# Tap 0 of a causal convolution on VectorE from PSUM, and one 128x1024 subtraction on GpSimd

## The chip, the cores and the metric

The kernel runs on one core of a Trainium2 chip. The metric is the device time of one execution in microseconds (us). Three runs of the kernel before took 265.92, 267.05 and 267.52 us, median 267.05 us.

The engines are TensorE (PE, matmuls; its weight loads are PEld), VectorE (DVE), ScalarE (ACT), GpSimd (POOL) and SyncE (SP, which here only issues DMAs). Each has its own instruction queue and runs it in order; they wait for each other through semaphores.

## The reference

For `x` of 4 batches x 1024 tokens x 256 features, with `xn = layernorm(x)`, the result is `x + ssm(xn) + ffn(xn)`:

```python
xz = xn @ W_in.T                      # 256 -> 1024 = 512 (x_inner) + 512 (z)
conv[t] = sum(cw[k] * x_inner[t - 3 + k] for k in 0..3) + conv_b    # causal, per channel
x_conv = silu(conv)
s_C = x_conv @ W_x[16:].T             # 512 -> 16
h[t] = 0.95 * h[t-1] + x_conv[t]      # a scan over the 1024 tokens
y = h * (s_C @ exp(B_log).T) * silu(z)
ssm = layernorm(xn + y @ W_out.T) * ln_g + ln_b
ffn = quantise_fp6_blocks(xn) @ quantise_fp6_blocks(W_ffn).T + bias
```

The 512 inner channels lie in four chunks of 128 partitions; a chunk of a batch is a tile of 128 channels x 1024 tokens. Nearly all matmuls are done in two or three parts, with each factor split in a rounded `hi` and a remainder `lo = value - hi`.

## The kernel before, in words

Batches are software-pipelined. `step(s)` (one such function per engine) writes out by hand the order in which an engine works on batch `here = s`, on the next one (`nxt`) and on the tail of the previous one (`prev`). Steps run from -1 to 4; for batches that don't exist nothing is emitted. The order is static, so what stands first in an engine's queue and waits holds back all behind it.

For each chunk `c` of a batch the work around the change is this:

- PE: `x_half(c)` puts the chunk's `x_inner` in a PSUM slot (128x1024; there are three slots, `SLOT_X` and `SLOT_Z` say which), `z_half(c)` does the same for `z`. Before PE overwrites a slot, `slot_free` makes it wait for the last reader.
- ACT, `taps` (L613): L628 writes `xc = cw[3] * x + conv_b` from PSUM (tap 3), L632 writes `tap0 = cw[0] * x` from PSUM to a buffer in SBUF.
- DVE, `conv_tap` (L995, the instruction is L997): adds tap 2 and then tap 1 to `xc`, each as one `scalar_tensor_tensor` that reads the PSUM slot and `xc` and writes `xc`.
- POOL, `conv_tap0` (L391, L395): adds the shifted `tap0` buffer to `xc`; this sets `conv_ready`.
- ACT, `silu_x` (L644): SiLU of `xc` in place. DVE, `scan` (L1026): the recurrence, `xc` to `hy`. POOL, `gate` (L403): `hy *= silu(z)`; `silu(z)` lies in a single buffer `sz`, which ACT (L639) refills for the next chunk when the gate is done.
- When all four chunks have their SiLU, PE makes `s_product` (L812), ACT and DVE split its result (`s_low`, L1032), PE makes `cb_product`, and DVE `y_product` (L1039) multiplies it into `hy`.
- ACT `y_high` (L658) rounds `y`; the low part is `y_low`: on POOL for the chunks in `YLO_POOL = (0, 1, 2)` (L412), on DVE for chunk 3 (L1046), and in the last batch also chunk 1 on DVE (`MOVED`). PE `out_tile(t)` (t = 0 to 7, 128 tokens each; L839 to L857) multiplies out both branches of a token tile; the first of a batch waits for all four low parts at L857.

Other work in the same queues: DVE has the token statistics (L934, L942, L949, L950), the quantisation (`quantise`, L980; `block_max`, L959; `block_scale`, L967), the low parts `xn_low` (L986) and `xd_low` (L992), `take` (L1061 and L1063), which takes an output tile out of PSUM, and `finish` (L1076), the last addition, after which SP stores half a batch. POOL has `rstd_1` (L383, L387), `rstd_2` (L431 to L436), `dequantise` (L425) and `scale_g` (L454). ACT has `normalise` (L595), `norm_2` (L689), `squares` (L668), `xn_high` (L603), `xd_high` (L610).

Inputs of an instruction lie in SBUF, except for the PSUM slots and the two PSUM output banks (`obank`). So L997, L1039, L1032, L986, L992, L1061 and L1063 read one operand from PSUM and one from SBUF; L1026, L980, L1046 and L1076 read two from SBUF, and so do POOL's 128x1024 instructions.

Of the kernel before, what the change touches and what calls it, by code (L numbers as in the profile page):

```python
# [40 lines left out]
ALU = mybir.AluOpType  # L41
# [9 lines left out]

FP8_SHIFT = 64.0

YLO_POOL = (0, 1, 2,)


def wait(eng, sem, count):
# [6 lines left out]
def build(nc, x, w_in, conv_w, conv_b, w_x, b_log, w_out, ln_g, ln_b, ffn_w, ffn_b, out):  # L64
# [13 lines left out]
    with ExitStack() as ctx:  # L78
# [44 lines left out]
        xn_lo = sb("xn_lo", [P, KM, SEQ], F32R)  # L123
        xd_hi = sb("xd_hi", [P, KM, SEQ], F32R)
        xd_lo = sb("xd_lo", [P, KM, SEQ], F32R)
        tap0 = sb("tap0", [P, 2, SEQ])
        xc = sb("xc", [P, NCH, SEQ])
        sz = sb("sz", [P, SEQ])
        hy = sb("hy", [P, NCH, SEQ])
# [167 lines left out]
        def first(b):  # L297
            return b == 0
# [69 lines left out]
        def _(pool):  # L368
# [19 lines left out]
                                   ALU.mult).then_inc(nmr1_ready, 1)  # L388

            @of_batch  # L390
            def conv_tap0(b, c):  # L391

                wait(pool, tap1_done, NCH * b + c + 1)
                n = SEQ - (TAPS - 1)
                pool.tensor_tensor(xc[:, c, TAPS - 1:], xc[:, c, TAPS - 1:], tap0[:, c % 2, 0:n],  # L395
                                   ALU.add).then_inc(conv_ready, 1)

            @of_batch
            def gate(b, c):

                wait(pool, scan_done, NCH * b + c + 1)
                wait(pool, sz_ready, NCH * b + c + 1)
                pool.tensor_tensor(hy[:, c, :], hy[:, c, :], sz[:, :], ALU.mult).then_inc(hsz_ready, 1)  # L403
# [98 lines left out]

            def step(s):
                prev, here, nxt = s - 1, s, s + 1
                conv_tap0(here, 2)
                conv_tap0(here, 3)
                gate(here, 1)
                rstd_1(nxt, 0)
                gate(here, 2)
                rstd_1(nxt, 1)  # L510
                rstd_2(prev, 0)
                dequantise(here, 0)
                gate(here, 3)
                scale_g(prev, 0)
                if first(here):
                    centre_w_out()
                dequantise(here, 1)
                if first(nxt):
                    prepare_b()
                    prepare_bias()  # L520
                y_low(here, 0)
                if first(here):
                    w_out_low()
                y_low(here, 1)
                y_low(here, 2)
                rstd_2(prev, 1)
                conv_tap0(nxt, 0)
                scale_g(prev, 1)
                conv_tap0(nxt, 1)
                gate(nxt, 0)  # L530

            every_step(step)
# [5 lines left out]
        def _(act):  # L538
# [73 lines left out]
            @of_batch  # L612
            def taps(b, c):  # L613
                if first(b):
                    if c == 0:
                        for i in range(2):
                            act.wait_ge(conv_loaded[i], 16)

                    if c == 2:
                        act.wait_ge(b_ready, 1)  # L620
                    if c == 3:
                        act.wait_ge(bias_ready, 1)
                wait(act, x_ready, NCH * b + c + 1)

                wait(act, s_ready, b)
                wait(act, scan_done, NCH * (b - 1) + c + 1)
                src = slot[SLOT_X[c]][:, :]
                act.activation(xc[:, c, :], src, ACT.Identity, bias=cb[:, c:c + 1],  # L628
                               scale=cw[:, c, TAPS - 1:TAPS]).then_inc(taps_ready, 1)

                wait(act, conv_ready, NCH * b + c - 1)
                act.activation(tap0[:, c % 2, :], src, ACT.Copy, scale=cw[:, c, 0:1]).then_inc(taps_ready, 1)  # L632

            @of_batch
            def silu_z(b, c):
# [107 lines left out]
        def _(pe):  # L743
# [124 lines left out]
            def step(s):  # L868
# [27 lines left out]
                x_half(nxt, 2)  # L896
                out_tile(here, 0)
                out_tile(here, 1)
                slot_free(nxt, (tap1_done, NCH * nxt + 1, nxt))
                z_half(nxt, 0)  # L900
                out_tile(here, 2)
                slot_free(nxt, (tap1_done, NCH * nxt + 2, nxt))
                x_half(nxt, 3)
                slot_free(nxt, (sz_ready, NCH * nxt + 1, nxt))
                z_half(nxt, 1)
# [1 line left out]
                out_tile(here, 4)  # L907
                slot_free(nxt, (sz_ready, NCH * nxt + 2, nxt))
                z_half(nxt, 2)
                slot_free(nxt, (tap1_done, NCH * nxt + 3, nxt))  # L910
                s_product(nxt)
                slot_free(nxt, (tap1_done, NCH * nxt + 4, nxt))
                z_half(nxt, 3)

            every_step(step)
# [2 lines left out]
        def _(dve):  # L918
# [82 lines left out]
            def conv_tap2(b, c):  # L1001
# [2 lines left out]
                        dve.wait_ge(conv_loaded[i], 16)  # L1004
                    dve.wait_ge(const_ready, 2)

                wait(dve, taps_ready, 2 * (NCH * b + c + 1))
                conv_tap(b, c, TAPS - 2, tap2_done)

            @of_batch  # L1010
            def conv_tap1(b, c):
                wait(dve, tap2_done, NCH * b + c + 1)
                conv_tap(b, c, TAPS - 3, tap1_done)

            @of_batch
            def scan(b, c):
# [108 lines left out]
            def step(s):  # L1125
# [37 lines left out]
                block_max(nxt, 1)  # L1163
                block_scale(nxt, 0)
                xd_low(here, 1)
                y_low(here, 3)
                finish(prev, 0)
                block_inverse(nxt, 0)
                if first(nxt):
                    w_in_low(1)  # L1170
                conv_tap2(nxt, 0)
                conv_tap1(nxt, 0)
                block_scale(nxt, 1)
                take_tile(here, 0)
# [62 lines left out]
```

## Time and profile before

| | us |
|---|---|
| median of three runs | 267.05 (265.92 to 267.52) |
| the profiled execution | 264.35 |
| its span, first to last instruction | 262.5 |
| PE busy | 212.7 (81%) |
| DVE busy | 226.2 (86%) |
| ACT busy | 157.9 (60%) |
| POOL busy | 205.9 (78%) |

The profile is that of one execution. An instruction's duration in it runs from where it is started to where it is complete, including time in which it is held up on its way to memory. "Idle before" is time in which the engine stood waiting for a semaphore, with the engine and line that released it. Busy times of the engines overlap.

### The profile page before, as it was taken

What the parts mean: (1) busy time and instruction counts of PE and PEld (TensorE: products, weight loads), DVE (VectorE), ACT (ScalarE), POOL (GpSimd) and SP (SyncE); (2) the same over time, 40 slices, a digit from 0 to 9 for tenths busy, and PEclk for the clock granted to TensorE, in tenths of its full rate; (3) what the DMA queues carried; (4) which work ended last, traced back from release to release, by engine and by line L of the source; (5) the groups of instructions that cost most, each with busy time, mean ns of one, the idle gap of its engine ahead of it and who ended that gap; (6) DMA issues with size and microseconds to landing.
All of it is one profiled execution on the core that took longest, in us unless ns stands there. A gap on an engine that the chain in (4) does not pass through costs nothing.

```text
span 262.5 us, 3471 instructions
## 1 busy us (share of the span) xinstructions
PE 212.7 (81%) x1252; PEld 175.5 (67%) x1252; DVE 226.2 (86%) x304; ACT 157.9 (60%) x240; POOL 205.9 (78%) x131
## 2 busy tenths in 40 slices
PE   0459954887699999879999969979999898667960
PEld 0438833355589887668898918868988587557960
DVE  3799899998599899958999999598999999683455
ACT  2897391466956537657995347748966444555450
POOL 1328949999997789999689599999597989995262
PEclk9989998599999999999999979999999999959995
DMA  6965000000000000004112000000202000002204
GB/s 223 289 199 160 1 2 0 0 1 0 0 2 0 1 2 0 0 0 152 47 48 80 0 0 1 2 0 2 80 0 82 1 0 0 0 2 80 84 0 160
DMA packets 10777, 11.18 MB, mean 43 GB/s; under 512 B 648, under 2 KB 10120, under 8 KB 10760
## 3 DMA queue, kind: packets, MB, share of 16 engines
q1 hardware_dynamic: 9488, 9.96, 11.6%
q10 hardware_dynamic: 1272, 0.99, 1.4%
q8 instruction: 10, 0.16, 0.3%
q14 instruction: 7, 0.06, 0.1%
HBM read 6.76 MB, written 4.19 MB: 42 GB/s over the span
## 4 chain that ended last, share of the span: by engine, by line
POOL 35%; DVE 25%; PE 12%; ACT 11%; issue 10%; DMA 5%; POOLq 0%; ACTq 0%; DVEq 0%
POOL hy L403 12%; POOL xc L395 8%; POOL rstd L383 6%; DVE xc L997 5%; DVE hy L1026 4%; DMA y<-fx 3%; DVE fx L1076 3%; DVE y_lo L1046 3%; PE slot L754 2%; POOL xd L425 2%; ACT xn L595 2%; DVE bn L934 2%; DVE rs L1061 2%; PE obank L857 2%; PE obank L850 2%
## 5 line engine op out<-in xcount | busy, mean ns | idle before, releaser
L758 PE MATMUL slot<-xn_hi,w_in_lo 128*128 128x512 f32 x128 | 52.8, 412 | 8.5 <-DVE xn_lo L986 3.3
L395 POOL TENSOR_TENSOR xc<-xc,tap 128x1021 f32<-128x1021 f32 x16 | 46.1, 2881 | 13.9 <-DVE xc L997 13.9
L403 POOL TENSOR_TENSOR hy<-hy,sz 128x1024 f32<-128x1024 f32 x16 | 48.9, 3058 | 3.6 <-DVE hy L1026 2.3
L759 PE MATMUL slot<-xn_lo,w_in_hi 128*128 128x512 f32 x128 | 51.3, 401 | 0.0
L760 PE MATMUL slot<-xn_hi,w_in_hi 128*128 128x512 f32 x128 | 51.1, 399 | 0.0
L1026 DVE TENSOR_TENSOR_SCAN hy<-decay,xc 128x1024 f32<-128x1024 f32 x16 | 45.4, 2844 | 0.7 <-ACT xc L644 0.7
L997 DVE SCALAR_TENSOR_TENSOR xc<-slot,cw,xc 128x1023 f32<-128x1023 f32 (+1 forms) x32 | 40.2, 1265 | 1.6 <-ACT tap L632 1.1
L758 PEld LDWEIGHTS slot<-xn_hi,w_in_lo 128*128 128x128 f32 x128 | 24.5, 191 | 20.7 <-issue 4.7
L644 ACT ACTIVATE xc<-xc 128x1024 f32<-128x1024 f32 x16 | 17.0, 1060 | 29.9 <-POOL xc L395 29.9
L849 PE MATMUL obank<-w_out_lo,y_hi 128*128 128x256 f32 x128 | 32.0, 282 | 0.0
L850 PE MATMUL obank<-w_out_hi,y_hi 128*128 128x256 f32 x128 | 32.0, 282 | 0.0
L412 POOL TENSOR_TENSOR y_lo<-hy,y_hi 128x1024 fp32r<-128x1024 f32 x11 | 28.1, 2573 | 0.9 <-ACT y_hi L658 0.8
L760 PEld LDWEIGHTS slot<-xn_hi,w_in_hi 128*128 128x128 f32 x128 | 24.5, 192 | 6.1
L759 PEld LDWEIGHTS slot<-xn_lo,w_in_hi 128*128 128x128 f32 x128 | 24.5, 191 | 4.8
L628 ACT ACTIVATE xc<-slot,cb,cw 128x1024 f32<-128x1024 f32 x16 | 19.2, 1203 | 12.3 <-PE slot L760 12.3
L1061 DVE SCALAR_TENSOR_TENSOR rs<-x_in,rstd,obank 128x256 f32<-128x256 f32 x32 | 15.0, 470 | 12.6 <-PE obank L857 9.1
L849 PEld LDWEIGHTS obank<-w_out_lo,y_hi 128*128 128x128 f32 x128 | 24.5, 191 | 0.0
L850 PEld LDWEIGHTS obank<-w_out_hi,y_hi 128*128 128x128 f32 x128 | 24.4, 191 | 0.0
L595 ACT ACTIVATE xn<-x_in,nmr,rstd 128x256 f32<-128x256 f32 x32 | 16.5, 590 | 13.1 <-POOL nmr L387 12.9
L639 ACT ACTIVATE sz<-slot 128x1024 f32<-128x1024 f32 x16 | 16.4, 1025 | 11.5 <-POOL hy L403 11.2
L658 ACT ACTIVATE y_hi<-hy 128x1024 fp32r<-128x1024 f32 x16 | 16.4, 1049 | 10.8 <-PE obank L857 10.8
L383 POOL TENSOR_TENSOR rstd<-ve,minus_half 128x4 f32<-128x4 f32 x8 | 17.1, 2136 | 5.6 <-DVE ve L950 5.6
(106 smaller groups left out, 525.8 us busy)
## 6 DMA issues: line engine op xcount, KB each, us to landing
y<-fx SPq DMA_DIRECT2D x7, 512.0 KB, 2.9
x_in<-L_attn_x SPq DMA_DIRECT2D x3, 1024.0 KB, 5.6
x_in<-L_attn_x SPq DMA_DIRECT2D x2, 512.0 KB, 4.0
rs<-L_attn_W_in SPq DMA_DIRECT2D x2, 512.0 KB, 10.0
fx<-L_attn_W_out SPq DMA_DIRECT2D x1, 512.0 KB, 12.5
y<-fx SPq DMA_DIRECT2D x2, 256.0 KB, 2.1
fx<-L_ffn_weight ACTq DMA_DIRECT2D x1, 256.0 KB, 7.8
xc<-L_attn_B_log ACTq DMA_DIRECT2D x1, 256.0 KB
```

The source lines that it names most:

```text
L383: pool.tensor_tensor(rstd1[:, b % XS, cols], ve1[:, cols], minus_half[:, cols], ALU.pow).then_inc(rstd1_ready, 1)
L395: pool.tensor_tensor(xc[:, c, TAPS - 1:], xc[:, c, TAPS - 1:], tap0[:, c % 2, 0:n], ALU.add).then_inc(conv_ready, 1)
L403: pool.tensor_tensor(hy[:, c, :], hy[:, c, :], sz[:, :], ALU.mult).then_inc(hsz_ready, 1)
L412: pool.tensor_tensor(y_lo[:, c, :], hy[:, c, :], y_hi[:, c, :].bitcast(F32), ALU.subtract).then_inc(ylo_pool, 1)
L595: act.activation(xn[:, t, :], x_in[:, b % XS, t, :], ACT.Identity, bias=nmr1[:, b % XS, t:t + 1], scale=rstd1[:, b % XS, t:t + 1]).then_in ...
L758: pe.matmul(dst, w_lo, m_hi, start=first, stop=False)
L759: pe.matmul(dst, w_hi, m_lo, start=False, stop=False)
L760: return pe.matmul(dst, w_hi, m_hi, start=False, stop=last)
L849: pe.matmul(bank[:, 0:DM], y_hi[:, c, tok], w_out_lo[:, c, :], start=c == 0, stop=False)
L850: pe.matmul(bank[:, 0:DM], y_hi[:, c, tok], w_out_hi[:, c, :], start=False, stop=False)
L997: dve.scalar_tensor_tensor(xc[:, c, back:], slot[SLOT_X[c]][:, 0:SEQ - back], cw[:, c, k:k + 1], xc[:, c, back:], ALU.mult, ALU.add).then_ ...
L1026: dve.tensor_tensor_scan(hy[:, c, :], decay[:, 0:1].broadcast_to([P, SEQ]), xc[:, c, :], 0.0, ALU.mult, ALU.add).then_inc(scan_done, 1)
```

## The change

POOL's `conv_tap0`, ACT's product into the buffer `tap0` and the buffer itself go. DVE adds tap 0 as it adds taps 2 and 1: from the PSUM slot, behind tap 1 of the same chunk. Each of the four places in DVE's order where `conv_tap1` stands gets a `conv_tap0` behind it. PE's waits for a free slot are for `conv_ready` (tap 0 done) instead of `tap1_done`; DVE's tap 2 waits for one ACT instruction of its chunk instead of two. `y_low` of chunk 3 goes from DVE's order to POOL's, behind the three that are there. In the last batch chunk 1 stays on DVE.

```diff
-YLO_POOL = (0, 1, 2,)
+YLO_POOL = (0, 1, 2, 3)
...
             @of_batch
-            def conv_tap0(b, c):
-
-                wait(pool, tap1_done, NCH * b + c + 1)
-                n = SEQ - (TAPS - 1)
-                pool.tensor_tensor(xc[:, c, TAPS - 1:], xc[:, c, TAPS - 1:], tap0[:, c % 2, 0:n],
-                                   ALU.add).then_inc(conv_ready, 1)
...
             def step(s):                                   # POOL
                 prev, here, nxt = s - 1, s, s + 1
-                conv_tap0(here, 2)
-                conv_tap0(here, 3)
                 gate(here, 1)
                 rstd_1(nxt, 0)
                 gate(here, 2)
...
                 y_low(here, 1)
                 y_low(here, 2)
+                y_low(here, 3)
                 rstd_2(prev, 1)
-                conv_tap0(nxt, 0)
                 scale_g(prev, 1)
-                conv_tap0(nxt, 1)
                 gate(nxt, 0)
...
                                scale=cw[:, c, TAPS - 1:TAPS]).then_inc(taps_ready, 1)
-
-                wait(act, conv_ready, NCH * b + c - 1)
-                act.activation(tap0[:, c % 2, :], src, ACT.Copy, scale=cw[:, c, 0:1]).then_inc(taps_ready, 1)
...
-                slot_free(nxt, (tap1_done, NCH * nxt + 1, nxt))     # PE, and so at 3 more places
+                slot_free(nxt, (conv_ready, NCH * nxt + 1, nxt))
...
-                wait(dve, taps_ready, 2 * (NCH * b + c + 1))
+                wait(dve, taps_ready, NCH * b + c + 1)
                 conv_tap(b, c, TAPS - 2, tap2_done)
...
+            @of_batch
+            def conv_tap0(b, c):
+                wait(dve, tap1_done, NCH * b + c + 1)
+                conv_tap(b, c, TAPS - 4, conv_ready)
...
                 conv_tap1(here, 2)                          # DVE's step
+                conv_tap0(here, 2)
                 conv_tap2(here, 3)
                 conv_tap1(here, 3)
+                conv_tap0(here, 3)
                 mean_var(nxt, 0)
                 scan(here, 1)
                 take_tile(prev, 3)
...
                 xd_low(here, 1)
-                y_low(here, 3)
                 finish(prev, 0)
...
                 conv_tap1(nxt, 0)
+                conv_tap0(nxt, 0)
                 block_scale(nxt, 1)
                 take_tile(here, 0)
                 conv_tap2(nxt, 1)
                 conv_tap1(nxt, 1)
+                conv_tap0(nxt, 1)
```

## Rows read from the trace of the kernel before

**Rows 1.** The page: busy time by engine, and the chain that ended last by engine.
```profile
PE 212.7 (81%) x1252; PEld 175.5 (67%) x1252; DVE 226.2 (86%) x304; ACT 157.9 (60%) x240; POOL 205.9 (78%) x131
...
POOL 35%; DVE 25%; PE 12%; ACT 11%; issue 10%; DMA 5%; POOLq 0%; ACTq 0%; DVEq 0%
```
**Rows 2.** Windows, from the end of one batch's last `xd_low` to the next's (busy us per engine).
```profile
72.72:126.15 53.43, 50.41 (x314) 42.45 (x312) 48.32 (x70) 32.47 (x45) 47.39 (x25) 1.00 0.07 21
126.15:182.07 55.92, 51.47 (x314) 42.78 (x312) 52.01 (x71) 37.10 (x58) 48.56 (x28) 0.97 0.06 19
182.07:232.73 50.66, 43.84 (x274) 36.98 (x272) 47.24 (x45) 30.99 (x48) 44.16 (x23) 0.96 0.06 22
```
**Rows 3.** Groups by line and form, whole run (xcount, busy us, mean ns, idle before).
```profile
L395 POOL TENSOR_TENSOR xc<-xc,tap 128x1021 f32<-128x1021 f32 x16 | 46.1, 2881 | 13.9 <-DVE xc L997 13.9
L997 DVE SCALAR_TENSOR_TENSOR xc<-slot,cw,xc 128x1022 f32<-128x1022 f32 x16 | 20.4, 1275 | 0.5
L632 ACT ACTIVATE tap<-slot,cw 128x1024 f32<-128x1024 f32 x16 | 17.8, 1112 | 0.0
```
**Rows 4.** Timeline of POOL (start, duration, xcount).
```profile
120.29 7.13 POOL L412 TENSOR_TENSOR y_lo<-hy,y_hi 128x1024 fp32r<-128x1024 f32 x3 [0.26 <-ACT y_hi L658]
...
146.55 1.99 POOL L395 TENSOR_TENSOR xc<-xc,tap 128x1021 f32<-128x1021 f32 x1 [2.51 <-DVE xc L997]
149.06 4.05 POOL L395 TENSOR_TENSOR xc<-xc,tap 128x1021 f32<-128x1021 f32 x1 [0.52 <-DVE xc L997]
153.06 4.35 POOL L403 TENSOR_TENSOR hy<-hy,sz 128x1024 f32<-128x1024 f32 x1
...
162.17 2.99 POOL L383 TENSOR_TENSOR rstd<-ve,minus_half 128x4 f32<-128x4 f32 x1
```
**Rows 5.** Timeline of DVE from the end of one batch's `xd_low` (126.15) to the next's.
```profile
126.15 2.35 DVE L1046 TENSOR_TENSOR y_lo<-hy,y_hi 128x1024 fp32r<-128x1024 f32 x1
128.43 1.21 DVE L1076 TENSOR_TENSOR fx<-fx,rs 128x1024 f32<-128x1024 f32 x1
...
136.17 2.73 DVE L1026 TENSOR_TENSOR_SCAN hy<-decay,xc 128x1024 f32<-128x1024 f32 x1
...
139.53 2.24 DVE L1076 TENSOR_TENSOR fx<-fx,rs 128x1024 f32<-128x1024 f32 x1
...
145.22 3.76 DVE L997 SCALAR_TENSOR_TENSOR xc<-slot,cw,xc 128x1022 f32<-128x1022 f32 x3
...
149.03 2.29 DVE L1026 TENSOR_TENSOR_SCAN hy<-decay,xc 128x1024 f32<-128x1024 f32 x1
...
151.94 3.32 DVE L1026 TENSOR_TENSOR_SCAN hy<-decay,xc 128x1024 f32<-128x1024 f32 x1
...
156.89 1.61 DVE L980 TENSOR_TENSOR xq<-xn,sinv 128x1024 fp8e4<-128x1024 f32 x1
...
161.63 2.74 DVE L1026 TENSOR_TENSOR_SCAN hy<-decay,xc 128x1024 f32<-128x1024 f32 x1
...
170.47 1.22 DVE L986 TENSOR_TENSOR xn_lo<-slot,xn_hi 128x1024 fp32r<-128x1024 f32 x1 [2.73 <-ACT xn_hi L603]
...
178.03 1.23 DVE L992 TENSOR_TENSOR xd_lo<-slot,xd_hi 128x1024 fp32r<-128x1024 f32 x1 [0.78 <-ACT xd_hi L610]
```
**Rows 6.** Timeline of PE: `out_tile(0)` at its first low part, and `s_product`.
```profile
130.94 0.63 PE L857 MATMUL obank<-w_out_hi,y_lo 128*128 128x256 f32 x4
...
154.34 3.31 PE L812 MATMUL slot<-xc,w_x_t 128*32 128x512 f32 x16 [2.60 <-ACT xc L644]
```
**Rows 7.** Timeline of DVE, fourth scans of the first and last batch.
```profile
53.58 3.51 DVE L1026 TENSOR_TENSOR_SCAN hy<-decay,xc 128x1024 f32<-128x1024 f32 x1
...
215.76 2.63 DVE L1026 TENSOR_TENSOR_SCAN hy<-decay,xc 128x1024 f32<-128x1024 f32 x1
```
**Rows 8.** Timeline of PE, `out_tile(2)` of the last batch.
```profile
240.25 0.38 PE L839 MATMUL obank<-bias_rows,ones_r 128*128 128x256 f32 x1 [1.38 <-DVE fx L1063]
```

More of the change, by code:

```diff
@@ L125, in build @@
         xd_lo = sb("xd_lo", [P, KM, SEQ], F32R)
-        tap0 = sb("tap0", [P, 2, SEQ])
         xc = sb("xc", [P, NCH, SEQ])
@@ L390, in conv_tap0 @@
             @of_batch
-            def conv_tap0(b, c):
-                wait(pool, tap1_done, NCH * b + c + 1)
-                n = SEQ - (TAPS - 1)
-                pool.tensor_tensor(xc[:, c, TAPS - 1:], xc[:, c, TAPS - 1:], tap0[:, c % 2, 0:n],
-                                   ALU.add).then_inc(conv_ready, 1)
-            @of_batch
             def gate(b, c):
@@ L898, in step @@
                 out_tile(here, 1)
-                slot_free(nxt, (tap1_done, NCH * nxt + 1, nxt))
+                slot_free(nxt, (conv_ready, NCH * nxt + 1, nxt))
                 z_half(nxt, 0)
                 out_tile(here, 2)
-                slot_free(nxt, (tap1_done, NCH * nxt + 2, nxt))
+                slot_free(nxt, (conv_ready, NCH * nxt + 2, nxt))
                 x_half(nxt, 3)
@@ L909, in step @@
                 z_half(nxt, 2)
-                slot_free(nxt, (tap1_done, NCH * nxt + 3, nxt))
+                slot_free(nxt, (conv_ready, NCH * nxt + 3, nxt))
                 s_product(nxt)
-                slot_free(nxt, (tap1_done, NCH * nxt + 4, nxt))
+                slot_free(nxt, (conv_ready, NCH * nxt + 4, nxt))
                 z_half(nxt, 3)
```

## The prediction, made before the changed kernel ran

> **What bounds the kernel now.** I read the page's shares first, then windows one batch long, then the timelines of DVE and POOL side by side. DVE is the busiest engine, yet POOL holds the largest share of the chain that ended last [rows 1]. The windows say that no engine leaves a batch much room: of the steady batch's 55.92 us DVE is busy 52.0, PE 51.5, POOL 48.6, ACT 37.1 [rows 2]. DVE's only longer idle spells in it are 2.73 and 0.78 us [rows 5]. So from 126.15 to past the fourth scan DVE never waits for a semaphore for more than a fraction of a microsecond, and what it is given more there, it does later.
>
> The side-by-side timelines show what busy hides. At 149.03 DVE starts a scan of 2.29 us; POOL's addition of tap 0, started at 149.06, takes 4.05 us, where the one before it took 1.99 [rows 4, 5]. It ends at 153.1, and the scan that starts meanwhile, at 151.94, takes 3.32 instead of 2.29, so it ran only from 153.1 on. The gate of 153.06 takes 4.35: it ran behind that scan. These instructions exclude each other: DVE's with two operands in SBUF, and POOL's. Three taps in a row with one PSUM operand took 3.76 us, 1.25 each [rows 5], while POOL's 1.99 us one ran beside them [rows 4]: they neither wait nor block. When both engines have something waiting, they take turns. The Trainium skill ("SBUF — State Buffer", section "Who interferes with whom") has the same split, one SBUF input or two, and a lock for the whole instruction; by that rule alone tap 0 on DVE is free of the lock.
>
> Read like this, the steady batch has on DVE 46.2 us of work at its own pace, 5.4 of lock waits (1.3 at y_low, 0.5 at scan 0, 1.1 at finish, 1.1 at scan 2, 0.4 at quantise, 0.5 at scan 3, 0.5 at a small L967) and 4.3 of idle, gaps under 0.4 included, which make 55.9.
>
> **The change part by part.** ACT loses 16 products of 1.11 us [rows 3]: nothing, ACT is not late, and tap 2 waited for it once. POOL loses four additions per batch, 2.0 us each when undisturbed (46.1 us with waits over the run, [rows 3]) and gains one y_low of 2.38 (7.13/3, [rows 4]). DVE gains four taps per batch: 1.22 each from start to start, +4.9. That form exists only with 1022 and 1023 columns, at 1.275 us [rows 3]; 1021 columns from the same PSUM slot can hardly differ, bounds 1.2 and 1.28. DVE loses y_low: 1.15 of work (the 2.35 less 1.2 of waiting, [rows 5]). Net DVE work +3.7 per batch, 49.9.
>
> Now the order, on the clock of the steady batch. *At 126.15*, in y_low's place, finish stands; POOL is in its third y_low until 127.42 [rows 4], so finish waits as y_low did, until 128.5. POOL's fourth y_low gets the lock behind it, 128.5 to 130.9. PE needs it at 130.94 [rows 6]: cost nothing, but with no margin. DVE: inverse, three taps of chunk 0 to 132.5; `take(0)` ends at 133.35, about where it did, since the store that it waits for starts a microsecond earlier. Three taps of chunk 1 to 137.0, scan 0 from 137.3 to 139.5 with POOL's scale_g done (before: 136.17 to 138.83, 0.5 of it waiting). *The first new collision*: the gate of chunk 0 starts at 139.6, as soon as the scan is done, while DVE is in a take; finish wants the lock at 140.2 and gets it at 141.9, ends 143.0. Before, POOL's tap 0 stood there and finish ended at 141.7: +1.3.
>
> Then statistics, take, and six taps where there were four: +2.4, scan 1 from 152.85 to 155.05 instead of 149.03: +3.8. ACT's SiLU of chunk 3 is ready at 153.85 instead of 154.2, so s_product, which waited 2.60 us for it [rows 6], starts 0.4 earlier; that helps nobody, since what follows on PE needs DVE's s_low. *Second collision*: gate 1 runs 155.1 to 157.45, so scan 2 ends at 159.65 (before 155.2: +4.5). POOL's rstd follows to 161.0, gate 2 from there to 163.4. *Third*: quantise wants the lock at 161.36 and gets it at 163.4, 2.0 of waiting where it had 0.4 [rows 5]. The two quantise and s_low end at 167.0 instead of 160.9: +6.1, and PE, which had s_low in time before, now waits some 4. Take; scan 3 waits 0.85 for rstd_2's power and ends at 170.75 (before 164.3): +6.5. The three y_product end at 174.15. DVE idled 2.73 us here for ACT's xn_high, itself behind POOL's rstd, which had waited for scan 3 (2.99 for a 1.0 us job) [rows 4, 5]. That idle time takes up part: xn_low starts 174.15 instead of 170.47, +3.7, and by `xn_low(1)`, which now follows PE's transposes of half 1 behind `out_tile(6)`, +4.1. From there `out_tile(7)`, y_high, xd_high and xd_low come in a chain, each +4.1. **So a steady batch costs 4.1 more**, lock waits 7.4 instead of 5.4.
>
> The others. Start up to the first batch's last xd_low: four more taps are +4.9, and no y_low goes yet; scans 1 and 2 stand back to back there, and without POOL's tap 0 between them save 1.8; scan 3 ends at 60.2 instead of 57.0 [rows 7], and rstd, gate 3 and the centring of W_out, queued on POOL behind it, carry +3.3 on to xd_low. Second batch: as the steady one without the finish collision, 4.1 - 0.35 = +3.75. Last batch: scan 3 (215.76, ended 218.3 [rows 7]) ends at 224.4; out_tile(7) +5.8; fourth y_low holds out_tile(0) of the tail at 241.5, +5.5; but out_tile(2) had waited 1.38 us for take(0) behind a store [rows 8], and goes from 240.25 to 244.2: +4.0, and the rest of the tail is as it was. **Sum: 3.3 + 3.75 + 4.1 + 4.0 = +15.2 us.** The profiled execution took 264.35, so 279.5 on its scale; the median of the runs is 2.7 above it, so 282.2 there. A walk like this lets no wait heal that it doesn't see; I take off 1 and say 281.
>
> **The rivals.** *A, the added work is all that counts, lock waits stay at 5.4.* DVE then has 49.9 + 5.4 = 55.3 and the 4.3 of idle shrink to near 1: 56.3, +0.4 a batch, some +2 with the start: 269. For it: POOL's lock time falls. Against: gates now start the moment their scan ends, exactly where DVE's next locked instruction comes.
>
> *B, faster: the lock is the bound and gets room.* In the steady batch POOL holds it some 38 us (48.6 of busy time [rows 2] less 10 of waiting inside its rows, as 2.0 each in those of 149.06 and 153.06 [rows 4]), DVE 14.6 (four scans of 2.2, five others of 1.15): 52.6 of 55.9. After, 38 - 8 + 2.4 + 13.4 = 45.8. If lock waits and idle on DVE together fall from 9.7 to under 6.0 (55.9 - 49.9), the kernel gets faster; that is the point from which it decides. Were they to fall to 3, a batch would take 52.9, about PE's own busy time [rows 2]: -3.0 in each of three and a half, 257. The place would be scans 2 and 3 and finish. For it: the sum above, and POOL's 35% of the chain [rows 1]. Against: DVE stands on the chain behind the locks too, and its six taps come in one block before scan 1, with POOL idle for 11 us meanwhile (141.9 to 155.1). The Trainium skill ("Perfetto Trace Analysis", section "Optimizing GPSIMD Operations") says to prefer other engines to GpSimd; followed here it gives this case. Its section "Optimizing Scalar/DVE Operations" says that a saturated DVE wants work taken off, and that is the forecast.
>
> *C, slower still: out_tile(0) waits.* If y_low 3 loses one more turn of the lock (1.15) or comes behind two, PE is 1.2 to 2.4 late at 130.94, of which take(0) has 1.1 of slack: +0 to 1.3 a batch, 286.
>
> **How the numbers follow.** Forecast 0.60, on its own 274 to 287 (each collision off by one turn of 1.2 to 2.4 a batch either way). A 0.17, 266 to 273. B 0.15, 250 to 264. C 0.08, 283 to 290. The range 267 to 288 leaves out B, some of C and the edge of A. One per cent is 2.7 us, about what a measurement of this kernel can tell from no change. Slower by over 1% takes the forecast, C and half or so of A: 0.76; within 1% 0.10; faster 0.14.
>
> **What would show it.** Right: taps at 1.2 to 1.28 with three per chunk; quantise of the steady batches at 3 us instead of 1.61; finish at 2.9; scan 1 some 3.8 later after the statistics; the idle before xn_low gone; batch windows of about 60, 57 and 55 us. Each step is wrong by itself if its row is not longer. Wrong as a whole: if quantise beats gate 2 to the lock (a margin of 0.36 us) and that heals more than the turn I count, if batch windows stay at 56 (A) or fall (B), or if PE waits over a microsecond for a low part at L857 in each batch (C).

## The result, and the profile after

The changed kernel took 280.16 us (median of 5 runs, 279.51 to 281.48) against 267.05 (5 runs, 265.92 to 267.52): 1.052 times the time before (95% interval 1.048 to 1.056), slower. The forecast was 281, its range 267 to 288. The profiled execution took 281.48 us with a span of 279.7. That is the highest of its five runs, and the profiled 264.35 of before lies under all five of its timed ones, so the spans of the two traces differ by 17.2 us where the medians differ by 13.1. The terms below are terms of the traces. In the 51 later runs of the kernel before, taken beside the experiments, its time lay between 264.2 and 267.8, with medians of 265.0, 266.1 and 265.5 in the three sessions; so 13.1 is itself known to a microsecond or so. Three runs of the experiments that lie in a slower state, two of e3's ten and one of g2's four, are left out of the times below.

The page of the changed kernel, busy time by engine and the chain that ended last (answers to [rows 1]):

```profile
PE 218.7 (78%) x1252; PEld 181.2 (65%) x1252; DVE 245.8 (88%) x316; ACT 143.0 (51%) x224; POOL 162.7 (58%) x119
...
DVE 39%; POOL 22%; PE 21%; issue 11%; DMA 3%; ACT 3%; POOLq 0%; DVEq 0%; ACTq 0%
```

POOL lost 43 us of busy time, DVE gained 19.6, and the chain moved from POOL (35 to 22%) to DVE (25 to 39%). The windows between the last `xd_low` of one batch and of the next (answers to [rows 2]; span, then busy us of PE, PE's weight loads, DVE, ACT, POOL, granted clock of PE, DMA share, GB/s):

```profile
76.73:135.13 58.40, 52.62 (x314) 44.51 (x312) 54.78 (x73) 29.05 (x41) 35.69 (x22) 0.94 0.06 19
135.13:194.39 59.26, 51.27 (x314) 43.72 (x312) 57.55 (x75) 33.55 (x54) 38.14 (x25) 0.97 0.05 18
194.39:250.23 55.84, 45.51 (x274) 38.20 (x272) 53.45 (x49) 28.03 (x48) 32.87 (x21) 0.94 0.06 20
```

Against [rows 2] that is +4.0 us up to the first window (76.73 for 72.72), +5.0, +3.3 and +5.2 in the three windows, and -0.3 in the tail: 17.2. In the middle one DVE has 57.55 of 59.26 us busy.

The timeline of DVE in that window (start, duration, form, idle before; answers to [rows 5]; line numbers have moved: taps L982, scan L1016, `finish` L1066, `block_scale` L952, `quantise` L965, `xn_low` L971, `xd_low` L977, `y_product` L1029, `s_low` L1022):

```profile
135.13 2.37 DVE L1066 TENSOR_TENSOR fx<-fx,rs 128x1024 f32<-128x1024 f32 x1
...
137.68 3.81 DVE L982 SCALAR_TENSOR_TENSOR xc<-slot,cw,xc 128x1023 f32<-128x1023 f32 x3
141.40 0.17 DVE L952 TENSOR_SCALAR s<-amax 128x32 f32<-128x32 f32 x1
...
146.30 2.23 DVE L1016 TENSOR_TENSOR_SCAN hy<-decay,xc 128x1024 f32<-128x1024 f32 x1
...
149.15 2.93 DVE L1066 TENSOR_TENSOR fx<-fx,rs 128x1024 f32<-128x1024 f32 x1
...
155.52 6.39 DVE L982 SCALAR_TENSOR_TENSOR xc<-slot,cw,xc 128x1022 f32<-128x1022 f32 x5
...
161.96 2.28 DVE L1016 TENSOR_TENSOR_SCAN hy<-decay,xc 128x1024 f32<-128x1024 f32 x1
...
164.87 3.99 DVE L1016 TENSOR_TENSOR_SCAN hy<-decay,xc 128x1024 f32<-128x1024 f32 x1
...
170.49 2.83 DVE L965 TENSOR_TENSOR xq<-xn,sinv 128x1024 fp8e4<-128x1024 f32 x1
...
176.38 2.28 DVE L1016 TENSOR_TENSOR_SCAN hy<-decay,xc 128x1024 f32<-128x1024 f32 x1
...
182.24 1.23 DVE L971 TENSOR_TENSOR xn_lo<-slot,xn_hi 128x1024 fp32r<-128x1024 f32 x1 [0.21 <-ACT xn_hi L591]
...
190.34 1.23 DVE L977 TENSOR_TENSOR xd_lo<-slot,xd_hi 128x1024 fp32r<-128x1024 f32 x1 [0.85 <-ACT xd_hi L598]
```

The reader is to see three things. Five taps stand in a row where there were three, at 1.28 us each (6.39 / 5). `finish` (2.93 for 2.24), scan 2 (3.99 for 3.32) and the first `quantise` (2.83 for 1.61) are longer though they compute what they did: they stand behind POOL. And the idle time before `xn_low` has gone from 2.73 to 0.21.

The timeline of POOL beside it (answers to [rows 4]; gate L394, y_low L403, `rstd_1` L382):

```profile
129.27 10.48 POOL L403 TENSOR_TENSOR y_lo<-hy,y_hi 128x1024 fp32r<-128x1024 f32 x4 [1.34 <-ACT y_hi L643]
...
148.60 2.39 POOL L394 TENSOR_TENSOR hy<-hy,sz 128x1024 f32<-128x1024 f32 x1 [2.65 <-DVE hy L1016]
164.32 2.39 POOL L394 TENSOR_TENSOR hy<-hy,sz 128x1024 f32<-128x1024 f32 x1 [13.33 <-DVE hy L1016]
166.67 2.99 POOL L382 TENSOR_TENSOR rstd<-ve,minus_half 128x4 f32<-128x4 f32 x1
169.74 0.20 POOL L386 TENSOR_TENSOR nmr<-nm,rstd 128x4 f32<-128x4 f32 x1
169.89 2.35 POOL L394 TENSOR_TENSOR hy<-hy,sz 128x1024 f32<-128x1024 f32 x1
```

In all three places POOL's gate starts some 0.5 us ahead of DVE's next instruction with two operands in SBUF: 148.60 against `finish` at 149.15, 164.32 against scan 2 at 164.87, 169.89 against `quantise` at 170.49. The first two gates start the moment DVE's scan before them is done; the third starts when `rstd_1` is done, which had itself waited for scan 2 (2.99 us for 1.0). Ahead of gate 1, while DVE does its taps, POOL stands still for 13.33 us.

### The profile page after: what moved, and what is told of

It reads as the page before. It is cut to its first block, busy times and chain, and to the rows that moved or that the text cites. A ratio compares the mean times of both kernels' runs of the same rounds, so it can differ in the third digit from the quotient of the medians.

```text
span 279.7 us, 3455 instructions
## 1 busy us (share of the span) xinstructions
PE 218.7 (78%) x1252; PEld 181.2 (65%) x1252; DVE 245.8 (88%) x316; ACT 143.0 (51%) x224; POOL 162.7 (58%) x119
## 4 chain that ended last, share of the span: by engine, by line
DVE 39%; POOL 22%; PE 21%; issue 11%; DMA 3%; ACT 3%; POOLq 0%; DVEq 0%; ACTq 0%
DVE xc L982 12%; DVE hy L1016 10%; POOL y_lo L403 6%; POOL hy L394 6%; DMA fx<-L_ffn_weight 3%; PE slot L739 2%; DVE fx L1066 2%; PE slot L808 2%; PE slot L743 2%; PE slot L744 2%; POOL xd L416 2%; PE slot L745 2%; DVE rs L1051 2%; PE obank L842 2%; PE slot L809 2%
## 5 line engine op out<-in xcount | busy, mean ns | idle before, releaser
L394 POOL TENSOR_TENSOR hy<-hy,sz 128x1024 f32<-128x1024 f32 x16 | 40.9, 2558 | 71.9 <-DVE hy L1016 71.7
L743 PE MATMUL slot<-xn_hi,w_in_lo 128*128 128x512 f32 x128 | 53.8, 420 | 10.4 <-DVE xn_lo L971 4.0
L982 DVE SCALAR_TENSOR_TENSOR xc<-slot,cw,xc 128x1023 f32<-128x1023 f32 (+2 forms) x48 | 60.6, 1271 | 1.0
L744 PE MATMUL slot<-xn_lo,w_in_hi 128*128 128x512 f32 x128 | 52.1, 407 | 0.0
L745 PE MATMUL slot<-xn_hi,w_in_hi 128*128 128x512 f32 x128 | 51.9, 405 | 0.0
L1016 DVE TENSOR_TENSOR_SCAN hy<-decay,xc 128x1024 f32<-128x1024 f32 x16 | 44.1, 2760 | 0.0
L403 POOL TENSOR_TENSOR y_lo<-hy,y_hi 128x1024 fp32r<-128x1024 f32 x15 | 39.1, 2636 | 4.2 <-ACT y_hi L643 4.1
L743 PEld LDWEIGHTS slot<-xn_hi,w_in_lo 128*128 128x128 f32 x128 | 25.1, 196 | 22.6 <-DVE xn_lo L971 4.8
L808 PE MATMUL slot<-s_lo,b_t 128*128 128x512 f32 x32 | 16.9, 527 | 17.3 <-DVE s_lo L1022 17.0
L643 ACT ACTIVATE y_hi<-hy 128x1024 fp32r<-128x1024 f32 x16 | 16.4, 1051 | 13.2 <-PE obank L842 13.2
L382 POOL TENSOR_TENSOR rstd<-ve,minus_half 128x4 f32<-128x4 f32 x8 | 16.9, 2114 | 8.3 <-DVE ve L935 8.3
```

The source lines that it names most:

```text
L403: pool.tensor_tensor(y_lo[:, c, :], hy[:, c, :], y_hi[:, c, :].bitcast(F32), ALU.subtract).then_inc(ylo_pool, 1)
L743: pe.matmul(dst, w_lo, m_hi, start=first, stop=False)
L744: pe.matmul(dst, w_hi, m_lo, start=False, stop=False)
L745: return pe.matmul(dst, w_hi, m_hi, start=False, stop=last)
L808: pe.matmul(slot[SLOT_CB[c]][:, half(g)], b_t[:, c * P:(c + 1) * P], s_lo[:, half(g)], start=True, stop=False)
L982: dve.scalar_tensor_tensor(xc[:, c, back:], slot[SLOT_X[c]][:, 0:SEQ - back], cw[:, c, k:k + 1], xc[:, c, back:], ALU.mult, ALU.add).then_ ...
```

## The experiments

In the expectations W is the theory of the prediction: DVE's queue pays every added instruction, and pays for the lock where the walk along the queues says so. A is its rival A: only the amount of work on DVE counts. R puts the loss into the other half of the change, y_low on POOL.

**e1 and e2: each half alone.** e1 is the kernel after with `y_low(here, 3)` back on DVE; e2 the kernel before with it on POOL.

```diff
-YLO_POOL = (0, 1, 2, 3)      # e1, against after; e2 is the reverse, against before
+YLO_POOL = (0, 1, 2,)
-                y_low(here, 3)                              # POOL's step
+                y_low(here, 3)                              # DVE's step, ahead of finish(prev, 0)
```

> The changed kernel with one half taken back: y_low of chunk 3 is on DVE again, tap 0 stays on DVE from PSUM. Theory W (DVE's queue is the bound; what it gets is paid in full, and lock waits fall where the order puts a locked DVE instruction behind one of POOL): y_low costs DVE 1.15 us more per batch than the changed kernel's finish alone, but L952 of the second batch (2.04 us, 1.9 of it behind POOL's fourth y_low) and PE's wait of 1.1 us for that low part fall away. Together 279 to 282 us, ratio to before 1.045 to 1.055: the tap carries the whole loss. Rival R (fourth y_low on POOL is what hurts, out_tile(0) comes late): most of the loss goes, 268 to 272 us, ratio 1.00 to 1.02.

> The kernel before with only the other half of the change: y_low of chunk 3 on POOL, tap 0 as it was (ACT product, POOL addition). Theory W: in the steady batches finish takes over the 1.2 us lock wait of y_low and DVE saves 1.15 us, but scan 0 still waits for SiLU 0 behind POOL, so 0 there; second batch +1 (small instruction L967 and out_tile(0) behind the fourth y_low). 266.5 to 269 us, ratio 0.998 to 1.008. Rival R: 272 to 278 us, ratio 1.02 to 1.04, with over 1 us of waiting for a low part in front of out_tile(0) in each batch.

Measured: e1 286.5 us, ratio 1.079 (1.073 to 1.084); e2 269.0, 1.015 (1.011 to 1.019). R falls: tap 0 is the costly half, y_low on POOL a small loss alone. But both are above what W allowed, e1 by 4.5 us and e2 by 0.7 points. In e2's trace, scan 0 of the steady batch takes 3.64 us where it took 2.73, and in its second batch `take(0)` waits 3.35 for PE, which has to wait for POOL's fourth low part: R's mechanism, at a small size. The halves don't add: 7.9% and 1.5% alone, 5.2% together. With tap 0 on DVE the second half is worth 2.7 points. In e1's steady batch (64.0 us for 59.26) the timelines of DVE and POOL show why (`block_scale` is L951, `y_product` L1028, `xn_low` L970, `scale_g` L445):

```profile
139.43 2.22 DVE L951 TENSOR_SCALAR s<-amax 128x32 f32<-128x32 f32 x1
...
181.50 1.23 DVE L1028 TENSOR_TENSOR hy<-slot,hy 128x1024 f32<-128x1024 f32 x1 [0.47 <-PE slot L808]
183.81 1.23 DVE L970 TENSOR_TENSOR xn_lo<-slot,xn_hi 128x1024 fp32r<-128x1024 f32 x1 [1.08 <-ACT xn_hi L590]
```

```profile
139.21 2.41 POOL L445 TENSOR_TENSOR rs<-rs,g_row 128x1024 f32<-128x1024 f32 x1 [2.20 <-ACT rs L673]
```

y_low itself costs 1.1. It puts `block_scale`, 0.17 us of work, right behind POOL's `scale_g`: 2.05 more. And 1.5 go at `y_product`, which waits for PE, and `xn_low`, which waits for ACT's `xn_high` and through it for PE (ACT waits 1.86 for it). PE runs slower there, as a window of e1 shows (same columns as above):

```profile
176.00:182.00 6.00, 6.00 (x16) 4.73 (x17) 5.53 (x6) 4.58 (x9) 5.84 (x6) 0.50 0.01 3
```

Having waited 3.2 us for `s_low`, and 3.7 for ACT's SiLU before, PE gets a granted clock of 0.50, the lower level, 1.2 GHz, for `cb_product` (0.94 in the six microseconds before, 0.99 in the six after). The sum is 4.65, nearly all of e1's 4.74 over the changed kernel in this batch.

**e3: no tap 0 anywhere.** The output lacks tap 0; everything else is as after.

```diff
-                conv_tap0(here, 2)       # and so for here, 3; nxt, 0; nxt, 1, in DVE's step
...
-                conv_tap(b, c, TAPS - 3, tap1_done)
+                conv_tap(b, c, TAPS - 3, conv_ready)
```

> The changed kernel without tap 0 of the convolution on any engine (the result lacks that tap; SiLU, the scans and PE's slots follow tap 1). Theory W: DVE loses four taps of 1.25 us per batch, but scan 0 still waits for POOL's scale_g and SiLU 0 (0.5 us sooner instead of 2.5), and the same collisions at finish, scan 2 and quantise stay; so -2.9 us per batch, -10 in all: 270 us, range 267 to 273, ratio 1.00 to 1.02. That is: even with tap 0 for nothing this order does not beat the kernel before. Rival A (only the added work counts): -5.0 per batch in full, 260 to 263 us, ratio 0.975 to 0.985.

Measured: 264.1 us against 264.95 for the kernel before in the same session, ratio 0.997 by these medians and 0.999 (0.995 to 1.003) over all ten runs: no difference that could be told from noise. That is below W's range (267 to 273) and above A's (260 to 263), so neither theory had the size. The timeline of DVE in its steady batch:

```profile
131.82 3.64 DVE L1016 TENSOR_TENSOR_SCAN hy<-decay,xc 128x1024 f32<-128x1024 f32 x1 [0.21 <-ACT xc L629]
...
136.09 2.92 DVE L1066 TENSOR_TENSOR fx<-fx,rs 128x1024 f32<-128x1024 f32 x1
...
149.17 3.99 DVE L1016 TENSOR_TENSOR_SCAN hy<-decay,xc 128x1024 f32<-128x1024 f32 x1
...
154.79 2.85 DVE L965 TENSOR_TENSOR xq<-xn,sinv 128x1024 fp8e4<-128x1024 f32 x1
```

All three collisions are there at full size without any tap 0. They come from gates that start at once, not from the taps. The batch takes 56.4 us, 2.8 less than after; the four taps cost 5.1 by their durations. Some 2 us of each batch's tap work therefore lie beside waits that are there anyhow, and the rows name them: scan 0 takes 3.64 here where it took 2.23 after, since without the taps DVE reaches it while POOL is still in `scale_g` (130.91 to 133.31), and DVE is idle for 2.4 us instead of 1.7. e3 is also the floor from which tap 0 can be priced on either engine, with y_low on POOL in all three: on POOL (e2) it adds 1.6 points of the time before and 1.0 us to the steady batch (57.4 for 56.4), on DVE (the changed kernel) 5.3 points and 2.8 us.

**e4: another order on DVE.** Work with a PSUM operand, or one operand, stands behind each scan, and both `quantise` between the `y_product`s; ACT does `silu_z(3)` ahead of `normalise(nxt, 0)`.

```diff
                 scan(here, 1)
                 take_tile(prev, 3)
-                scan(here, 2)
                 token_stats(nxt, 1)
                 aggregate(nxt, 1)
-                quantise(here, 0)
                 mean_var(nxt, 1)
-                quantise(here, 1)
+                scan(here, 2)
                 s_low(here)
                 take_tile(prev, 4)
                 scan(here, 3)
                 y_product(here, 0)
+                quantise(here, 0)
                 y_product(here, 1)
+                quantise(here, 1)
                 y_product(here, 2)
```

> The changed kernel with DVE's order between the scans written otherwise: scan 1, take(3), token statistics, aggregate and mean_var of half 1 (no lock, 2.4 us, as long as gate 1), scan 2, s_low, take(4) (no lock, while gate 2 runs), scan 3, y_product 0, quantise 0, y_product 1, quantise 1, y_product 2; on ACT silu_z 3 stands ahead of normalise 0. Same work on every engine. Theory W with the lock: scan 2 and quantise 0 no longer wait 1.7 us each, y_product 0 comes some 3 us sooner; lock waits of the steady batch go from 6.9 to some 4.5 us; -1.5 to -3 us a batch: 270 to 275 us, ratio 1.01 to 1.03. Rival A (lock waits don't matter, DVE's work is the same): no change, 279 to 281 us, ratio 1.047 to 1.055.

Measured: 281.2 us, 1.062 (1.057 to 1.067): no gain, where W had expected 270 to 275. The timeline of DVE:

```profile
167.74 2.29 DVE L1016 TENSOR_TENSOR_SCAN hy<-decay,xc 128x1024 f32<-128x1024 f32 x1
...
175.70 1.21 DVE L965 TENSOR_TENSOR xq<-xn,sinv 128x1024 fp8e4<-128x1024 f32 x1
...
184.27 1.23 DVE L971 TENSOR_TENSOR xn_lo<-slot,xn_hi 128x1024 fp32r<-128x1024 f32 x1 [3.96 <-ACT xn_hi L591]
```

The waits at scan 2 (2.29 for 3.99) and `quantise` (1.21 for 2.83) are gone. But ACT's `normalise` overwrites what `quantise` reads, so it comes late, `norm_2` and `xn_high` behind it, and DVE idles 3.96 before `xn_low`. The gain was lost to a wait that my order made, so e4 decides nothing between W and A by its time. Its steady batch (60.4 us) has 2.65 us less of DVE busy than after, for the same work, and 3.8 more of idle.

**f4: a second order.** Both `quantise` ahead of scan 1, the statistics between scans 1 and 2, `s_low` behind scan 2; on ACT `xn_high(nxt, 0)` ahead of `norm_2(prev, 0)`.

```diff
+                quantise(here, 0)
+                quantise(here, 1)
                 scan(here, 1)
                 take_tile(prev, 3)
-                scan(here, 2)
                 token_stats(nxt, 1)
                 aggregate(nxt, 1)
-                quantise(here, 0)
                 mean_var(nxt, 1)
-                quantise(here, 1)
+                scan(here, 2)
                 s_low(here)
```

> The changed kernel with DVE's order written otherwise, and the ACT swap of the run f3 in it: both quantise ahead of scan 1, where POOL idles and no lock is taken; scan 1, take(3), statistics, aggregate and mean_var of half 1, scan 2, s_low, take(4), scan 3, the three y_product. Same work. The first reordering (quantise behind scan 3) moved the y_products 2.7 us forward but made ACT's normalise, norm_2 and xn_high late by as much, since normalise waits for quantise; here it does not. Theory W: lock waits of the steady batch fall from 6.9 to some 3.7, s_low comes 3 us sooner and PE's clock stays up; -3 us a batch: 268 to 272 us, ratio 1.01 to 1.03. Rival A (only the amount of DVE's work counts): 279 to 281, 1.047 to 1.06.

Measured: 275.3 us, 1.034 (1.028 to 1.040), 5 us under the changed kernel, between W's 268 to 272 and A's 279 to 281. The timeline of DVE:

```profile
157.92 2.35 DVE L965 TENSOR_TENSOR xq<-xn,sinv 128x1024 fp8e4<-128x1024 f32 x2
160.19 2.28 DVE L1016 TENSOR_TENSOR_SCAN hy<-decay,xc 128x1024 f32<-128x1024 f32 x1
...
165.12 2.28 DVE L1016 TENSOR_TENSOR_SCAN hy<-decay,xc 128x1024 f32<-128x1024 f32 x1
...
169.16 2.85 DVE L1016 TENSOR_TENSOR_SCAN hy<-decay,xc 128x1024 f32<-128x1024 f32 x1
...
185.96 2.21 DVE L952 TENSOR_SCALAR s<-amax 128x32 f32<-128x32 f32 x1
```

Scan 2 and `quantise` wait for nothing, DVE's work is the same, and the kernel is faster. In the steady batch (58.1 us for 59.3) DVE's busy time fell by 1.20 and its idle time stayed (1.76 for 1.71), so the gain is lock waits that went: they were real time, and A is not all. But 3.4 us of waits were taken away there (1.8 at scan 2, 1.6 at `quantise`) and 1.15 gained: 0.6 came back at scan 3 (2.85 for 2.28) and 1.5 at `block_scale` (2.21 for 0.73), which is why W had expected too much. f4 carries ACT's swap too, which on the kernel before (f3) is worth 0.6%; what it is worth here no run separates. The steady batch still takes 2.2 more than before.

**f1 and f2: tap 0 on DVE for two chunks.** f1 has it there for chunks 0 and 1, f2 for chunks 2 and 3; the other two are on POOL with ACT's product as before. y_low is as after.

```diff
+TAP0_POOL = (2, 3)           # f1; (0, 1) in f2
...
             def conv_tap0(b, c):                            # DVE's; POOL has one for the others
+                if c in TAP0_POOL:
+                    return
                 wait(dve, tap1_done, NCH * b + c + 1)
```

> The changed kernel with tap 0 of chunks 2 and 3 back on ACT and POOL (PE's slots of these chunks follow tap 1 again); chunks 0 and 1 on DVE, fourth y_low on POOL. Theory W: up to the statistics as the changed kernel (finish waits 1.7 us behind gate 0, +1.3 against the kernel before), after them as the kernel before (scan 1 ahead of POOL's tap 0 of chunk 3, quantise waits 0.4, and s_low comes early, so no clock loss on PE): steady batch 57.3 us where the changed kernel has 59.3; 271 to 274 us, ratio 1.022 to 1.034. Rival A (each of the 16 taps costs the same, two per batch are taken off): half of the loss between no tap (265) and four (280): 272 to 273 us too, so this run alone does not tell them apart; its pair does.

> The changed kernel with tap 0 of chunks 0 and 1 back on ACT and POOL (DVE's tap 0 of chunk 2 waits besides for POOL's of chunk 1, long done); chunks 2 and 3 on DVE. Theory W: finish loses its 1.7 us behind gate 0, but the two taps ahead of scan 1 stand in the stretch in which DVE never idles, and scan 2 and quantise wait as in the changed kernel, and s_low is late: steady batch 58 to 58.6 us; 276 to 279 us, ratio 1.04 to 1.052, so the pair of chunks 2 and 3 carries most of the loss. Rival A: the same as for chunks 0 and 1 on DVE, 272 to 273 us.

Measured: f1 272.3 us, 1.024 (1.017 to 1.032); f2 274.9, 1.034 (1.028 to 1.040). (f2 has a further wait on DVE, for POOL's chunk before its own, long past when it is reached.) DVE's timelines, f1 first:

```profile
157.74 3.31 DVE L1037 TENSOR_TENSOR_SCAN hy<-decay,xc 128x1024 f32<-128x1024 f32 x1
...
162.69 1.61 DVE L984 TENSOR_TENSOR xq<-xn,sinv 128x1024 fp8e4<-128x1024 f32 x1
...
176.25 1.23 DVE L990 TENSOR_TENSOR xn_lo<-slot,xn_hi 128x1024 fp32r<-128x1024 f32 x1 [2.73 <-ACT xn_hi L607]
```

```profile
158.70 3.99 DVE L1038 TENSOR_TENSOR_SCAN hy<-decay,xc 128x1024 f32<-128x1024 f32 x1
...
164.33 2.84 DVE L984 TENSOR_TENSOR xq<-xn,sinv 128x1024 fp8e4<-128x1024 f32 x1
...
176.18 1.22 DVE L990 TENSOR_TENSOR xn_lo<-slot,xn_hi 128x1024 fp32r<-128x1024 f32 x1 [0.30 <-ACT xn_hi L607]
```

Each has two more taps on DVE per batch. f1 keeps POOL's additions for chunks 2 and 3 and with them the rows of before (3.31, 1.61, idle 2.73); its steady batch takes 57.2 us, 57.3 expected. f2 has the rows of after and 58.4. The same work costs 1.2 us a batch more at the place that pushes the gates into scan 2 and `quantise`. A had the two equal at 272 to 273. All four runs of f2 (274.5 to 276.8) lie above all four of f1 (271.5 to 274.4), though narrowly, and the two intervals overlap. f2's total is 1 us under W's range and 2 us over A's. The split goes W's way, with about half the size that W gave it.

**f3: the kernel before with ACT's swap.**

```diff
-                norm_2(prev, 0)
                 xn_high(nxt, 0)
+                norm_2(prev, 0)
                 xn_high(nxt, 1)
```

> The kernel before with one swap on ACT: xn_high of half 0 stands ahead of norm_2(prev, 0) instead of behind it. In its steady batch DVE idles 2.73 us for xn_high 0, which stands behind 2.06 us of norm_2 on ACT. Theory W (DVE's queue sets the batch, and this is its idle time): xn_low 0 comes 2 us sooner, take(5) frees the output bank sooner, out_tile(7) too; -1.5 to -2 us in the second and third batch, nothing in the first: 261 to 263.5 us, ratio 0.98 to 0.993. Rival (PE or POOL sets the batch): no change, 0.997 to 1.003.

Measured: 264.4 us (12 runs, 263.42 to 265.78), 0.994 (0.990 to 0.997): with g1 below the fastest kernel with the full result, ahead of before and after, though W had expected 261 to 263.5. The timeline of DVE:

```profile
169.38 1.23 DVE L986 TENSOR_TENSOR xn_lo<-slot,xn_hi 128x1024 fp32r<-128x1024 f32 x1 [0.76 <-ACT xn_hi L603]
...
179.21 2.21 DVE L967 TENSOR_SCALAR s<-amax 128x32 f32<-128x32 f32 x1
```

The idle time before `xn_low` fell by 2.0 (2.73 to 0.76), and 1.5 of it was given back 10 us later: DVE now reaches `block_scale` while POOL is in a y_low (2.21 us for 0.73).

**g1 and g2: `block_scale` behind the last `xd_low`**, added to f3 and to f4.

```diff
-                block_scale(nxt, 0)
                 xd_low(here, 1)
+                block_scale(nxt, 0)
```

> The kernel f3 (the kernel before with xn_high 0 ahead of norm_2 on ACT) with one more swap, on DVE: block_scale of half 0, a 128x32 instruction of 0.17 us, goes behind xd_low 1. In f3 it got into the shadow of POOL's y_low and took 2.21 and 2.36 us, with xd_low 1 behind it, which gave back 1.6 of the 2 us that the ACT swap had won. Theory W: xd_low 1 starts some 1.7 us sooner in batches 2 and 3, PE's x_half with it; block_scale then waits for the lock just ahead of y_low, which would wait there anyway: 259.5 to 262.5 us, ratio 0.976 to 0.988. Rival (the small instruction's 2.2 us is a reading of the trace and not time lost): as f3, 0.990 to 0.997.

> The same DVE swap in the run f4 (the changed kernel reordered), whose block_scale of half 0 also took 2.2 to 2.3 us. Theory W: 1.5 us less in batches 2 and 3, 270.5 to 273.5 us, ratio 1.018 to 1.030; it stays above the kernel before, since DVE still has 3.7 us more work in a batch of which it idles hardly any. Rival: as f4, 1.03 to 1.04.

Measured: g1 264.5 us, 0.996 (0.993 to 0.999); g2 276.3, 1.041 (1.033 to 1.049). Neither gained on its base: W was wrong about both, and the numbers are about those of its rival (0.990 to 0.997, and 1.03 to 1.04). The timelines of DVE and POOL in g1:

```profile
123.25 1.23 DVE L992 TENSOR_TENSOR xd_lo<-slot,xd_hi 128x1024 fp32r<-128x1024 f32 x1 [0.30 <-ACT xd_hi L610]
124.39 3.21 DVE L967 TENSOR_SCALAR s<-amax 128x32 f32<-128x32 f32 x1
127.52 1.21 DVE L1046 TENSOR_TENSOR y_lo<-hy,y_hi 128x1024 fp32r<-128x1024 f32 x1
```

```profile
120.43 7.14 POOL L412 TENSOR_TENSOR y_lo<-hy,y_hi 128x1024 fp32r<-128x1024 f32 x3
```

`xd_low` comes before `block_scale`, and the wait stands behind it. DVE gets nothing in before POOL's three y_low are over at 127.57. It is through with `finish` 9.4 us after the burst began (129.80), in the same batch of f3 9.3 us (130.47 from 121.21). For what follows on DVE, POOL's burst sets the time. The rival had called the 2.2 us a mere reading of the trace; the rows rather show the wait going to whatever DVE has next with a claim on the lock (in g1's steady batch y_low takes 3.50 at 180.71).

## Why the prediction was right, step by step

**Right as a mechanism.** The trace shows the walk's three collisions where it put them. `finish` took 2.93 us (predicted 2.8), `quantise` 2.83 (predicted 3), scan 2 ran 3.99 behind gate 1. Tap 0 took 1.281 us each (bounds 1.2 and 1.28). Scan 1 stood 3.95 later in the window (26.83 us after its start for 22.88; predicted 3.8). PE waited 5.6 us for `s_low`, where before it had not waited. On busy time the steady batch now has about 6.9 us of lock waits (1.2 and 1.8 at `finish`, 1.8 at scan 2, 1.6 at `quantise`, 0.5 at `block_scale`) where 7.4 were predicted and 5.4 stood before, and 1.7 of idle. Those waits are time and not only wider rows: f4 removed two of them and gained a third of their length, f1 and f2 moved them at equal work. But of the ranges that W gave for the ten runs only that of f1 held. e1, e2, e3, f2, f3 and f4 went its way by another amount, and e4, g1 and g2 brought no gain where it had expected one; in f3, f4, g1 and g2 the rows show why, a wait that was taken away turned up again at another instruction. The experiments show what costs time and where, and not that a walk like this gets the size.

One reading of the prediction is a slip: it has POOL idle for 11 us from 141.9 to 155.1, which is 13.2 (measured 13.33).

The row of the taps is what the Trainium skill ("SBUF — State Buffer", section "Who interferes with whom") would have: with one SBUF input they don't contend. The row that shows it is the one at 137.68, three taps in 3.81 us (1.27 each) while POOL's y_low run until 139.75; the five in a row kept to 1.28 too, but POOL stood idle beside them. The same section counts `tensor_scalar` among the instructions that can take the shared pair when their operands meet the conditions for it; the trace agrees, with 0.17 us of work taking 2.22 (e1) and 3.21 (g1) beside POOL's 128x1024.

**The terms.** The sum was 3.3 + 3.75 + 4.1 + 4.0 = 15.2 us; the traces have 4.0 + 5.0 + 3.3 + 4.9 = 17.2, and the medians 13.1. On its own scale the changed kernel's trace is 281.5 where the walk gave 279.5; that the median came within 0.9 us of the forecast owes something to its lying 1.3 under the profiled run, where I had added 2.7 for the opposite and taken off 1. Luck is in the sum as well: with the late start of the trace taken off (below), two of the four terms were too large and two too small, by about a microsecond each. And one cost in all of them was too small: the prediction took a tap as 1.22 us from start to start. From the start of the block of taps to scan 1 it was 3.81 us with three taps (145.22 to 149.03, [rows 5]) and 6.44 with five (155.52 to 161.96), so an added one costs 1.31 and four of them 5.3 a batch, for the 4.9 in the sum. Of the four terms:

- *Start, +4.0 for 3.3.* Half of it is no effect of the change. The first tap already stood 2.1 us later, before anything of the change: a weight landed later (DVE's first use of it at 10.11 for 9.39), and parts of DVE's weight preparation took longer (1.53 and 1.55 us for 0.68 and 1.16). e1 is the same kernel up to its first y_low, and there the first tap starts at 24.53. These are the first taps of before, after and e1, from DVE's timelines:

```profile
24.39 2.59 DVE L997 SCALAR_TENSOR_TENSOR xc<-slot,cw,xc 128x1023 f32<-128x1023 f32 x2
26.45 3.90 DVE L982 SCALAR_TENSOR_TENSOR xc<-slot,cw,xc 128x1023 f32<-128x1023 f32 x3
24.53 3.90 DVE L981 SCALAR_TENSOR_TENSOR xc<-slot,cw,xc 128x1023 f32<-128x1023 f32 x3
```

  The last xd_low ends at 74.82 in e1, 2.1 us after that of before. So the term of the change is about 2, and 3.3 was too much. Scans 1 and 2 saved 1.8 together (4.46 for 6.22), as said. What the walk left out is that scan 0 had waits behind POOL's taps too, which went with them, 1.5 us in all; the rows of before and after:

```profile
32.30 2.98 DVE L1026 TENSOR_TENSOR_SCAN hy<-decay,xc 128x1024 f32<-128x1024 f32 x1 [0.74 <-ACT xc L644]
36.16 2.23 DVE L1016 TENSOR_TENSOR_SCAN hy<-decay,xc 128x1024 f32<-128x1024 f32 x1
```

- *Second batch, +5.0 for 3.75.* An omitted wait: with POOL's burst one y_low longer, `block_scale` there took 2.04 us for 0.17. DVE timeline:

```profile
80.72 2.04 DVE L952 TENSOR_SCALAR s<-amax 128x32 f32<-128x32 f32 x1
83.61 0.48 DVE L1051 SCALAR_TENSOR_TENSOR rs<-x_in,rstd,obank 128x256 f32<-128x256 f32 x1 [0.86 <-PE obank L842]
```

  The 0.86 is rival C: PE waited 1.08 us for the fourth low part (L842, 82.77) and `take(0)` for PE (0.40 before). It came in this batch of the changed kernel alone. The two waits come to 2.3, more than the 1.25 that the term was short of, so part of the 3.75 wasn't there; the prediction gives no working for the 0.35 by which it set this batch under the steady one.
- *Steady batch, +3.3 for 4.1.* The predicted wait of scan 3 for `rstd_2`'s power (0.85) did not come: scan 3 took 2.28 at 176.38, POOL's power 1.04 at 176.01. The step failed in a rule of mine, that the 128x4 power excludes a scan as the large instructions do. Without the 0.85 the walk has 3.25 for the measured 3.34.
- *Last batch with its tail, +4.9 for 4.0.* The healing at `out_tile(2)` came (it starts 6.39 us after the window's end, before 7.52), but DVE's next `finish` then waited 2.24 for `scale_g` (1.24 before) and `out_tile(4)` 0.62 behind it, so little stayed. Scan 3 of this batch took 3.87 us where it had taken 2.63, behind POOL's `dequantise`, which had started 0.2 us ahead of it.

**What the sum left out** and the trace has: the granted clock. After the 5.6 us wait for `s_low` it was 0.76 in 176 to 182, and L808's matmuls took 527 ns on average where the same ones took 405 before. In the steady batch no `y_product` waited for it; in the second one waited 0.47 for PE; in e1 it was part of 1.5.

**The rivals.** A (269) and B (257) are out. The idle time shrank as A had it (3.9 to 1.7, on busy time), but lock waits grew. For B lock waits and idle had to fall under 6.0; they are 8.6. POOL did get room, 13.33 us idle in one piece, and none of it at a time when DVE wanted the lock. Here a rule of the Trainium skill can be weighed again ("Perfetto Trace Analysis", section "Optimizing GPSIMD Operations"): to prefer other engines to GpSimd. In this kernel following it cost 5.2%, and against e3 tap 0 is about three times dearer on DVE than it was on GpSimd.

**Still open.** The difference of the traces exceeds that of the medians by 4 us. Half of it is the late start; the other half I put down to the two executions as well (the profiled 264.35 of before lies under the medians of its later runs), and no run shows it. How much of f4's gain is ACT's swap, and why POOL's burst let no turn go in g1, stays open too.

## What to carry to other kernels

An engine with few idle microseconds pays added work nearly in full, even where the work itself conflicts with nothing; an engine with many but at the wrong times, like POOL here, gives little of its relief back: some 3.3 us at the start of this kernel, while in the steady batch the lock waits grew. Work that two engines exclude each other from is to be read as a sequence: taking one of POOL's instructions away lets the next start at once, and what counts is which of DVE's it then meets. Before moving work, price it where it is, by a kernel without it: four additions of 2 us cost 1.0 us a batch on POOL, four taps of 1.28 us cost 2.8 on DVE.

## What the runs showed of the hardware

- A tiny instruction can wait as long as a large one: a 128x32 TENSOR_SCALAR of 0.17 us took 2.04 to 2.36 behind one 128x1024 instruction of POOL (after, e1, f3, f4), and 3.21 when it lost its turn (g1). The trace shows this as duration, not as idle time.
- Turns are usual and not certain. Mostly DVE got in after POOL's current instruction; once, in g1 at 124.39, it asked during the second of POOL's three y_low, and the third followed without a turn for DVE (7.14 us, 2.38 each).
- POOL's power on 128x4 waits for a scan (2.99 us for 1.0 at 166.67, with scan 2 running from 166.7) but one that has already begun held none up in two cases: those of 176.01 and 115.76 ran on while scan 3 kept its 2.28.
